# A state-space layer and a routed low-rank projection on one core: the set-up re-ordered, pair 0's projection put among the weights

## What is computed

```python
# x: (64 sequences, 64 heads, 1024 samples); per head a kernel K of 1024 samples from 64 modes
dtA = (-exp(log_A_real) + 1j * A_imag) * exp(log_dt)[:, None]
K   = 2 * einsum('hn,hnl->hl', Cc * (exp(dtA) - 1) / A, exp(dtA * arange(L))).real
y   = (causal convolution of (x * mask) with K) + x * mask * D      # mask: sample < length of the sequence
x   = x + y * mask
# then per token (sequence, head): 1024 -> 1024, plus a low-rank part of 8 experts of rank 16
logits  = x @ Wr.T + 5 * onehot(language)
gates   = softmax of the two largest logits, 0 elsewhere
out = x + x @ W.T + 2 * einsum('bter,bte,eor->bto', x @ A.T, gates, B)
```

## Time and profile before

| | us |
|---|---|
| the runs, median of 3 | 696.15 (695.85 to 696.51) |
| the profiled execution | 695.72 |
| its span, first to last instruction | 693.9 |
| PE busy | 645.8 (93%) |
| DVE busy | 490.0 (71%) |
| ACT busy | 467.8 (67%) |
| POOL busy | 20.4 (3%) |

### The profile page before, as it was taken

One profiled execution on the slowest core, in us unless ns is written; L12 is line 12 of the kernel. 1 busy time (PEld: TensorE's weight loads), 2 busy tenths in 40 slices (PEclk: granted clock), 3 DMA queues, 4 the chain that ended last, 5 costly groups with the idle time before them and its releaser, 6 DMA issues.

```text
span 693.9 us, 12598 instructions
## 1 busy us (share of the span) xinstructions
PE 645.8 (93%) x3621; PEld 615.2 (89%) x3621; DVE 490.0 (71%) x1531; ACT 467.8 (67%) x973; POOL 20.4 (3%) x46
## 2 busy tenths in 40 slices
PE   3364999999999999999999999999999999999997
PEld 2353899999999999999999999999999999999997
DVE  8876567777776767777776767777776767777621
ACT  4784577677768677677768677777768677675411
POOL 2000000000000000000000000000000000000000
PEclk9875899999999999999999999999999999999999
DMA  7123023222123233223123233223123223221112
GB/s 241 49 69 89 11 68 70 54 52 68 32 67 68 68 68 68 53 53 68 31 68 68 68 68 68 53 53 68 31 68 68 68 68 68 53 53 39 31 32 60
DMA packets 22869, 43.36 MB, mean 62 GB/s; under 512 B 8104, under 2 KB 13512, under 8 KB 22856
## 3 DMA queue, kind: packets, MB, share of 16 engines
q1 hardware_dynamic: 17576, 26.42, 17.1%
q10 hardware_dynamic: 5280, 16.78, 9.5%
HBM read 26.35 MB, written 16.84 MB: 62 GB/s over the span
## 4 chain that ended last, share of the span: by engine, by line
DVE 36%; ACT 25%; issue 18%; PE 13%; ACTq 6%; DMA 2%; DVEq 1%; SPq 0%
DVE state L783 17%; PE pmg L1104 9%; ACTq L470 5%; ACT result L488 4%; ACT u_hi L416 4%; ACT turn L379 3%; ACT L393 3%; DVE y_lo L830 3%; ACT swapped L439 2%; ACT Z L405 2%; DVE Z L770 2%; ACT xt L413 2%; DVE c_lo L764 2%; ACT z_swap L398 2%; PE pc L1029 2%
## 5 line engine op out<-in xcount | busy, mean ns | idle before, releaser
L1104 PE MATMUL pmg<-w_hi,y_hi 128*128 128x388 f32 (+1 forms) x768 | 268.7, 350 | 1.7 <-ACT result L488 0.2
L1104 PE MATMUL pmg<-w_hi,y_lo 128*128 128x388 f32 (+1 forms) x768 | 260.1, 339 | 0.0
L1104 PE MATMUL pmg<-w_lo,y_hi 128*128 128x388 f32 (+1 forms) x768 | 259.8, 338 | 0.0
L1104 PEld LDWEIGHTS pmg<-w_hi,y_hi 128*128 128x128 f32 x768 | 144.3, 188 | 7.5 <-ACT result L488 6.5
L1104 PEld LDWEIGHTS pmg<-w_hi,y_lo 128*128 128x128 f32 x768 | 144.6, 188 | 0.2
L1104 PEld LDWEIGHTS pmg<-w_lo,y_hi 128*128 128x128 f32 x768 | 144.2, 188 | 0.0
L439 ACT ACTIVATE swapped<-state 64x128 f32<-64x128 f32 x192 | 59.3, 309 | 67.1 <-DVE state L783 65.7
L783 DVE SCALAR_TENSOR_TENSOR state<-swapped,scan_tab,state 128x192 f32<-128x192 f32 (+1 forms) x240 | 73.8, 349 | 12.1 <-ACT swapped L439 0.2
L812 DVE TENSOR_TENSOR s_lo<-state,s_hi 128x896 fp32r<-128x896 f32 x32 | 35.0, 1093 | 31.5 <-ACT s_hi L461 31.5
L744 DVE TENSOR_TENSOR u_lo<-xt,u_hi 128x1024 fp32r<-128x1024 f32 x32 | 39.2, 1225 | 24.8 <-ACT u_hi L416 24.8
L461 ACT ACTIVATE s_hi<-state 128x896 fp32r<-128x896 f32 x32 | 30.5, 953 | 35.0 <-DVE state L783 35.0
(11 more groups left out here) (195 smaller groups left out, 1068.1 us busy)
## 6 DMA issues: line engine op xcount, KB each, us to landing
rows<-in_x SPq DMA_DIRECT2D x64, 256.0 KB, 5.1
out<-result ACTq DMA_DIRECT2D x62, 256.0 KB, 3.0
toe<-kpad SPq DMA_DIRECT2D x32, 128.0 KB, 4.5
result<-in_L_cond_W SPq DMA_DIRECT2D x5, 512.0 KB, 7.2
rows<-in_L_cond_W SPq DMA_DIRECT2D x2, 512.0 KB, 7.8
result<-in_L_cond_A SPq DMA_DIRECT2D x1, 512.0 KB, 5.8
b_rows<-in_L_cond_B SPq DMA_DIRECT2D x1, 512.0 KB, 7.0
xt<-in_L_cond_W SPq DMA_DIRECT2D x1, 512.0 KB, 8.8
```

Of the source, the lines that this page charges most:

```text
L1104: ins = nc.tensor.matmul(pm[:, n, 0:c1 - c0], y[s][:, c, :], w[:, c, c0:c1], start=(c == 0 and y is y_hi and w is w_hi), stop=(c == CH - 1 ...
```

## The change

The set-up is written anew, and pairs 0 and 1 are taken out of the loop, which now begins with step 2 (`Fori(1, LOOPS)`); from there on all orders are the old ones.

- **Parameters.** The decay's exponential on DVE (14 steps among the others) becomes one exponential of ACT. The far tables move from behind the rows' split to behind the angles of duo 0 on DVE, and `k_first` behind the chunk factors.
- **Kernel samples of pairs 0 and 1.** Two small products of PE (`kernel_row`, with the one-hot columns of `pick`) sum the modes and give a row of samples; ACT copies it; it goes to its own DRAM tensor and comes back as two planes. Duo 0's Z2 is made in halves (`turn_first_powers`, `rotate_first_powers`).
- **Weights.** The order of the tiles is the rank weights, W6, W7, router, W0, W2, W1, W3, W4, W5, B; W2 and W4 are turned in `px`. W0 has its own buffer, W4 comes through `b_sorted`. B is sorted by one copy of ACT in place of eight of POOL, and is last.
- **Pair 0.** Bank 2 starts with three tiles to come, and is cut in 3, 3 and 2 chunks with tiles 7, 8 and 9 in between (`project` takes a range of chunks); bank 0 and bank 1 follow when their tiles are split. `control(0, 1)` moves behind bank 0, tile 10 into bank 1.
- **Peeled steps.** Each engine has a list of its own for the rest of pair 0 and for pair 1. On ACT `finish(0, 0)` stands before `split_rows(0, 2)`, and `finish(0, 1)` between `swap_odd(0, 3, 0)` and `split_obs(0, 4)`.
- **SP** loads rows one step further ahead (`load_rows(b, m + 4)`), and waits in `load_toe` for `tlo_ready` before `k_stored`.

The core of the diff; in the lists (from `store_row(0)` on) lines taken out are not shown again, they stand in the functions above.

```diff
-xt1_rows = xt[1][:, :, :].rearrange("p c t -> p (c t)")
-w_rows = [xt1_rows, rows[0][:, :], result[0][:, :], result[1][:, :], result[0][:, :], result[1][:, :],
-          rows[1][:, :], result[1][:, :]]
-a_rows = result[0][:, :]
+w0_rows = sb("w0_rows", [P, LEN])
 b_rows = sb("b_rows", [P, EXPERTS, 8, RANK])
 b_sorted = sb("b_sorted", [P, 8, EXPERTS, RANK])
+w_rows = [w0_rows[:, :], rows[0][:, :], result[0][:, :], result[1][:, :],
+          b_sorted[:, :, :, :].rearrange("p o e r -> p (o e r)"), result[0][:, :], rows[1][:, :], result[1][:, :]]
+a_rows = result[0][:, :]
...
-TILE = [(A_, in_pm, 0), (B_, in_pc, 0), (W_, in_pm, 6), (W_, in_pc, 0), (WR_, in_pm2, 0), (W_, in_pm, 7),
-        (W_, in_pc, 1), (W_, in_pm, 2), (W_, in_pc, 3), (W_, in_pm, 4), (W_, in_pc, 5)]
+TILE = [(A_, in_pm, 0), (W_, in_pc, 6), (W_, in_pm, 7), (WR_, in_pm2, 0), (W_, in_pm, 0), (W_, in_px, 2),
+        (W_, in_pc, 1), (W_, in_pm, 3), (W_, in_px, 4), (W_, in_pc, 5), (B_, in_pc, 0)]
...
+store_row(0)
+sp.wait_ge(pad_stored, 64)
+load_toe_rows(0)
+store_row(1)
+load_toe_rows(1)
+load_w(4)
+sp.dma_start(b_rows[:, :, :, :].rearrange("p e o r -> p e (o r)"),
+             B.rearrange("e (p o) r -> p e (o r)", o=8)).then_inc(b_in, 16)
 sp.wait_ge(wt_full, w_tile(7) + 1)
 load_w(3)
+sp.wait_ge(px_full, 2)
+load_rows(0, 3)
+sp.wait_ge(wt_full, w_tile(2) + 1)
+load_w(5)
 sp.wait_ge(wt_full, w_tile(1) + 1)
 load_rows(0, 2)
 store_kernel(0, 2)
...
+def turn_first_powers(j):
+    for h in (2 * j, 2 * j + 1):
+        ins = nc.scalar.activation(Z2[:, h, :], Z[:, h, :], ACT.Copy, scale=gen_scalar(C2_RE, 0, h, False))
+    ins.then_inc((z_half, z_swapped)[j], 1)
+def kernel_row(j):
+    act.wait_ge(row_full, j + 1)
+    nc.scalar.activation(k_row[j][:, :], row_psum[:, j, :], ACT.Copy).then_inc(k_ready, 1)
+def sort_b():
+    act.wait_ge(b_in, 16)
+    act.wait_ge(wt_full, w_tile(4) + 1)
+    nc.scalar.activation(b_sorted[:, :, :, :].rearrange("p o e r -> p e o r"), b_rows[:, :, :, :], ACT.Copy
+                         ).then_inc(b_ready, 1)
...
+turn_first_powers(0)
+split_ctr(0, 0)
+kernel_row(0)
+turn_first_powers(1)
 weight(0)
 turns_of(1, False)
+weight(1)
 copy_states(0, 0, first=True)
+split_ctr(0, 1)
+kernel_row(1)
 swap_odd(0, 0, 0)
+split_obs(0, 0, first=True)
 swap_odd(0, 0, 1)
+waves(1)
+swap_odd(0, 0, 2)
+split_toe(0, 0, toe_rows_back, first=True)
+split_states(0, 0, first=True)
 weight(2)
+split_rows(0, 1, first=True)
 weight(3)
 split_obs(0, 1, first=True)
+split_y(0, 0)
 weight(4)
 weight(5)
+weight(6)
+magnitudes(1, False, reused=True)
+weight(7)
+ratios(0, 0)
+weight(8)
+swap_powers(1)
+sort_b()
+weight(9)
+turn_powers(1, False)
+weight(10)
 copy_states(0, 1)
 swap_odd(0, 1, 0)
+split_gated(0, 0)
 swap_odd(0, 1, 1)
 swap_odd(0, 1, 2)
+split_toe(0, 1, toe_rows_back)
+split_states(0, 1)
+finish(0, 0)
+split_rows(0, 2)
 split_ctr(0, 2)
 split_obs(0, 2)
+split_y(0, 1)
+copy_states(0, 2)
+act.wait_ge(gen_staged, 1)
+turns_of(None, True)
+swap_odd(0, 2, 0)
+magnitudes(None, True)
+swap_odd(0, 2, 1)
+swap_odd(0, 2, 2)
+split_toe(0, 2)
+split_states(0, 2)
+split_ctr(0, 3)
+split_obs(0, 3)
+waves(2)
+split_rows(0, 3)
+swap_powers(2)
+turn_powers(2, True)
+nc.scalar.activation(warm[:, :], phase[:, 0:1], ACT.Exp)
+ratios(0, 1)
+split_y(0, 2)
+split_ctr(0, 4)
+split_gated(0, 1)
+copy_states(0, 3)
+swap_odd(0, 3, 0)
+finish(0, 1)
+split_obs(0, 4)
+swap_odd(0, 3, 1)
+split_toe(0, 3)
+swap_odd(0, 3, 2)
+split_states(0, 3)
+split_rows(0, 4)
...
+def rotate_first_powers(j):
+    dve.wait_ge((z_half, z_swapped)[j], 1)
+    for h in (2 * j, 2 * j + 1):
+        ins = vec.scalar_tensor_tensor(out=Z2[:, h, :], in0=z_swap[:, h, :],
+                                       scalar=gen_scalar(C2_IM, 0, h, False), in1=Z2[:, h, :],
+                                       op0=ALU.mult, op1=ALU.add)
+    ins.then_inc((z2_half, z2_ready)[j], 1)
...
+split_rows(0, 0)
+rotate_first_powers(0)
+split_ctr(0, 0, kernel=False)
+rotate_first_powers(1)
+low_weight(0)
+angles(1)
+low_weight(1)
+split_ctr(0, 1, kernel=False)
+dve.wait_ge(chunk_ready, 1)
+scanning = scan_states(0, 0, staged=False)
+next(scanning)
+next(scanning)
+split_obs(0, 0)
+next(scanning)
+next(scanning)
+split_toe(0, 0, toe_rows_back)
+split_states(0, 0)
+dve.wait_ge(small_in, 48)
+dve.wait_ge(consts, 4)
+vec.tensor_copy(len_f[:, :], len_i[:, :]).then_inc(masks, 1)
+vec.tensor_copy(lang_f[:, :], lang_i[:, :]).then_inc(masks, 1)
 dve.wait_ge(masks, 2)
 vec.tensor_tensor(valid[:, :, :], sample_no[:, :].unsqueeze(2).to_broadcast([P, CH, SEQS]),
                   len_f[:, :].unsqueeze(1).to_broadcast([P, CH, SEQS]), ALU.is_lt).then_inc(masks, 1)
 vec.tensor_scalar(bias[:, :], expert_no[:, :], lang_f[:, :], LANG_BIAS, ALU.is_equal, ALU.mult
                   ).then_inc(masks, 1)
 low_weight(2)
 low_weight(3)
+split_obs(0, 1)
+dve.wait_ge(masks, 4)
+merge(0, 0)
 split_rows(0, 1)
+split_y(0, 0)
 low_weight(4)
 low_weight(5)
+low_weight(6)
 powers(1)
+low_weight(7)
+route(0, 0)
+low_weight(8)
+low_weight(9)
+rotate_powers(1, False)
+low_weight(10)
 scanning = scan_states(0, 1, staged=False)
 next(scanning)
+next(scanning)
+split_gated(0, 0)
+next(scanning)
+next(scanning)
+split_toe(0, 1, toe_rows_back)
+split_states(0, 1)
+split_rows(0, 2)
 split_ctr(0, 2)
 split_obs(0, 2)
+merge(0, 1)
+split_y(0, 1)
+angles(2)
+dve.wait_ge(scan_staged, 1)
+scanning = scan_states(0, 2)
+next(scanning)
+next(scanning)
+next(scanning)
+next(scanning)
+split_toe(0, 2)
+split_states(0, 2)
+split_ctr(0, 3)
+split_obs(0, 3)
+split_rows(0, 3)
+powers(2)
+rotate_powers(2, True)
+route(0, 1)
+merge(0, 2)
+split_y(0, 2)
+split_ctr(0, 4)
+split_gated(0, 1)
+scanning = scan_states(0, 3)
+next(scanning)
+split_obs(0, 4)
+next(scanning)
+split_toe(0, 3)
+next(scanning)
+next(scanning)
+split_states(0, 3)
+split_rows(0, 4)
...
+def kernel_row(j):
+    pe.wait_ge((z2_half, z2_ready)[j], 1)
+    if j:
+        pe.wait_ge(k_ready, j)
+    for h in range(2):
+        ins = nc.tensor.matmul(row_psum[:, j, :], pick[:, h, :], Z2[:, 2 * j + h, :], start=h == 0,
+                               stop=h == 1, skip_group_check=True)
+    ins.then_inc(row_full, 1)
...
+def last_bank(b, m, tables_split, rows_ahead):
+    project(b, m, 2, 0, 2)
+    turn_gates(b, m, tables_split)
+    project(b, m, 2, 2, 5)
+    if rows_ahead:
+        turn_rows(b, m + 3)
+    project(b, m, 2, 5, 7)
+    add_loras(b, m)
+    project(b, m, 2, 7, 8)
+    add_lora(BANK_ORDER[2])
...
+kernel_row(0)
 pe.wait_ge(prm_ready, 2)
+turn_powers(0, 0, first=True)
 control(0, 0)
+kernel_row(1)
+pe.wait_ge(clo_ready, 1)
 turn_powers(0, 1)
 turn_weight(2)
+turn_rows(0, 1)
+pe.wait_ge(k_ready, 2)
 turn_weight(3)
+pe.wait_ge(wlo_ready, 2)
+convolve(0, 0, first=True)
 turn_weight(4)
+pe.wait_ge(uhi_ready, 2)
 turn_weight(5)
 pe.wait_ge(merged, 1)
 turn_weight(6)
+wait_y(0, 0)
+pe.wait_ge(wlo_ready, 4)
+project(0, 0, 0, 0, 3)
+turn_weight(7)
+project(0, 0, 0, 3, 6)
+turn_weight(8)
+project(0, 0, 0, 6, 8)
+turn_weight(9)
+pe.wait_ge(wlo_ready, w_tile(3) + 1)
+project(0, 0, 1)
+pe.wait_ge(wlo_ready, w_tile(4) + 1)
+control(0, 1)
+pe.wait_ge(wlo_ready, w_tile(5) + 1)
+project(0, 0, 2, 0, 2)
+turn_weight(10)
+turn_gates(0, 0, 2)
+project(0, 0, 2, 2, 5)
+turn_rows(0, 2)
+project(0, 0, 2, 5, 7)
+pe.wait_ge(wlo_ready, WTILES)
+add_loras(0, 0)
+project(0, 0, 2, 7, 8)
+add_lora(BANK_ORDER[2])
 turn_powers(0, 2)
+convolve(0, 1)
+control(0, 2)
+wait_y(0, 1)
+project(0, 1, 0)
+pe.wait_ge(clo_ready, 3)
+turn_powers(0, 3)
+project(0, 1, 1, 0, 5)
+turn_rows(0, 3)
+project(0, 1, 1, 5, 8)
+convolve(0, 2)
+control(0, 3)
+turn_powers(0, 4)
+last_bank(0, 1, 5, True)
...
```

More of the change, by code:

```diff
@@ L111, in cond_resid_kernel @@
         toe_back = [bass.AP(t[:, :, :].tensor, 2 * P - 2, [[2 * P, P], [1, 2], [-2, P]]) for t in toe]
+        k_row = [sb(f"k_row{s}", [2, P]) for s in range(2)]
+        toe_rows = [bass.AP(t[:, :, :].tensor, 0, [[2 * P, P], [P, 2], [1, P]]) for t in toe]
+        toe_rows_back = [bass.AP(t[:, :, :].tensor, P - 1, [[2 * P, P], [P, 2], [-1, P]]) for t in toe]
+        pick = sb("pick", [P, 2, 2])
         DT_RE, TURNS, C2_RE, C2_IM, A_RE, AA_RE, A_IM, AA_IM = range(8)
@@ L314, in _ @@
                     step(b, m)
-            step(LOOPS, 0)
+            step(LOOPS, 0, rows_left=False)
         @block.gpsimd
@@ L510, in _ @@
             waves(0)
+            act.wait_ge(far_step, 5)
+            for q in range(2):
+                nc.scalar.activation(far_wave[:, q, :, :], far_wave[:, q, :, :], ACT.Sin, scale=-TWO_PI,
+                                     bias=phase[:, 2 + q:3 + q]).then_inc(far_waved, 1)
             act.wait_ge(px_full, 1)
@@ L619, in _ @@
             dve.wait_ge(tables, 1)
+            for h in range(2):
+                vec.memset(pick[0:MODES, h, h:h + 1], 1.0)
             vec.tensor_scalar(phase[:, 2:4], phase[:, 0:2], TWO_PI, None, ALU.mult).then_inc(tables, 1)
@@ L1128, in _ @@
+            convolve(0, 0, first=True)
             turn_weight(4)
+            pe.wait_ge(uhi_ready, 2)
```

(30 more changed lines are left out.)

283 lines of the change are left out of this document (106 added, 177 removed).

## The result

The changed kernel takes 706.73 us, median of 4 runs (706.13 to 707.92), beside 696.33 us of 4 runs of the kernel before (695.85 to 697.55): ratio 1.0149, interval 1.013 to 1.0168. It is slower by 10.4 us. The forecast was 706.8.

A forecast was written before the change was run, and what follows sets the result against it. PE was taken to set the pace from 74.7 us; pair 2's first bank at 124.6 against 115.9 gave +8.7, the clock 2, sum +10.7 on 695.7: 706.4, with 0.4 to the median 706.8 us, range 698.8 to 713.0.

The forecast's parts named there:

- A: Set-up to the split of pair 0: about 5 us earlier, near half at 35.2 instead of 40.6, y split at 43.7.
- terms without a row: Costs no profile row priced: kernel-row product and its copy, taken 0.6 us; ACT's sort of B, taken 1.0.
- B: Pair 0's banks among the weights, 43.7 to 68.3 us: a PE stall of 3.0, pair 0 done 25.6 us earlier.
- C: From there to pair 1's first bank, at 79.9 us: a lead of 12.8 us over the kernel before.
- D: Peeled step 1 up to the rows of pair 3: a serial chain of ACT and DVE ending at 95.5 us.
- E: From the rows of pair 3 to pair 2's first bank: a serial chain to 124.6 us, +8.7 us at full clock.
- The clock, 2 us: PE's clock halving after gaps before the gates' turn and convolution 3: 2 us added, ends 0 and 4.
- Rival 3: PE cold all through step 1, its 23 us of work taking twice as long: about 715 us, chance 0.06.
- Rival 1: Peeled steps keep up and the 12.8 us lead stays, if PE stalls under 12.8 us: 683.4 us, chance 0.09.

The follow-up runs named there:

- experiment 7: experiment 6 with the kernel samples of pairs 0 and 1 made and sent the old way, as a column through `kpad`: 681.64 us, ratio 0.9787.
- experiment 1: The changed kernel with `finish(0, 1)` on ACT moved behind the rows of pair 4 (`split_rows(0, 4)`): 701.44 us, ratio 1.0063.
- experiment 2: The changed kernel with the tails of ACT's and DVE's peeled lists replaced by the loop's own step, PE's list kept: 695.63 us, ratio 0.999.
- experiment 4: The changed kernel with idle PE products in five gaps: 705.62 us; again with 11 instead of 24 before the gates' turn: 706.74 us.
- experiment 3: experiment 2 with `finish(0, 0)` on ACT also moved, behind the control and observation splits: 693.34 us, ratio 0.9954.
- experiment 6: experiment 5 with PE's wait for B's tile moved from before the loop into the step, before bank 0: 681.11 us, ratio 0.9777.
- experiment 5: The changed kernel's new set-up, but all 11 tiles before the first step, no early banks, loop from step 0: 685.89 us, ratio 0.9838.

## Why the prediction was right

- **A** (near half 35.2, bank 43.7): 34.95 and 43.87. Right; but I gave the rows of samples a share in it, and experiment 7 shows that they have none. Of the terms without a row, the products of one row of samples took 1.01 us and its copy 0.25, where I took 0.6 together, and the sort of B took 1.06, where I took 1.0. I also read the earlier trace rows a little wrong: the row is below 9 in slices 2 to 5 only, and not in the first or the last one. Nothing hangs on that.
- **B** (pair 0 done at 68.3, stall 3.0): stall 3.3, end 69.2. The 0.9 is a term that I had left out: the clock fell in that stall already (0.84 in the window at 63.0), the turn of rows took 1.94 us for 1.0, and the first few products behind it ran at half clock. None of the 0.9 reached the next mark.
- **C** (79.9): 80.03. Right, and the bank that began there ran at half clock till 84.
- **D** (95.5): 96.07. The Trainium skill, "ScalarE: Activation LUTs", section "What ACT_TABLE_LOAD costs", would have added a drain of 1.38 us. In the trace ACT's load of 1.28 us ends at 92.17 and the waves start at 92.19, so there is none to see:

```profile
90.89 1.28 ACT L415 ACT_TABLE_LOAD   x1
92.19 0.63 ACT L415 ACTIVATE angle<-angle 128x512 f32<-128x512 f32 x1
```

- **E** (99.9, 106.4, `zo_hi` at 115.4, bank at 124.6 plus the clock): 100.40, 106.91, 116.43, 127.05. The chain is right and experiments 1 and 2 show it by taking it away. The gates' turn is 0.5 us late, as all since D; pair 1's last bank then took 0.6 longer than 7.1 us, with half clock until 111.
- **The clock, 2 us.** As a total it fits: the far products took 2.4 us for 1.2, pair 1's end took 0.6 more, and from the first bank of pair 2 on, which began at half clock, it is 0.2 more than before. Its place was too narrow: I named two gaps, and the clock was low from 63 to 66.7 us, 77 to 84, 98 to 111 and 117 to 128. Rival 3, which put PE at half clock all through step 1, went too far as well: from 84 to 96 us the granted clock was 1.00. The rule of the Trainium skill, "TensorE: Matmul & The Clock Gate", section "HAM oscillation — how this bites in real kernels", agrees with these rows in kind: the clock fell four times, each time in or soon after a wait. But the price of it was small here, since what PE does at half speed lay mostly beside the chain of ACT and DVE.
- **Rival 1** decides at PE stalls of 12.8 us, and I counted 21.5 at full clock, 23.5 with the clock. By the marks the lead at 80.03 was 96.48 - 80.03 - 3.8 = 12.65, the lag at the end 11.1: 23.8 us were lost between. Only 1.94 + 2.86 + 3.89 + 5.54 + 1.56 = 15.8 of them are idle time in the brackets; the other 8.0 are mostly PE at half clock (by the distances of its products about 7.5), where it works while it would otherwise have waited. So the sum is right and its split was not: slow products stand in the place of waits, which is also why experiment 4 gained nothing by warming some of them. Experiment 2 has brackets of 1.5, 2.9 and 2.9 there, and its time comes out even with the kernel before.
- **The agreement to 0.1 us is in part luck.** The first bank of pair 2 came 0.45 us later than the sum with the clock has it (127.05 for 126.6), the profiled execution took 706.97 for 706.4, and the 2 us of the clock were a choice between 0 and 4. What the record supports is the mechanism and the size within about 1 us.
- **What I did not foresee** is the price of pair 0's early banks themselves. With the loop's order in step 1 they still end at 693.3, while the same set-up without them takes 681.1. The first bank of pair 2 starts at 113.96 in experiment 3 and at 101.46 in experiment 6, so the 12.6 us of span between them are lost before it: PE's waits are 15.1 us against 8.1, and the clock is 0.81 against 1.00 from 80 to 102 us. Where the waits come from, DVE's timelines tell; the first row of the scan of pair 1 in the kernel before, in the changed kernel and in experiment 5:

```profile
49.11 0.74 DVE L783 SCALAR_TENSOR_TENSOR state<-state,tab,px 128x192 f32<-128x192 f32 x2 [0.25 <-ACT swapped L439]
```

```profile
63.14 0.73 DVE L870 SCALAR_TENSOR_TENSOR state<-state,tab,px 128x192 f32<-128x192 f32 x2
```

```profile
46.79 0.73 DVE L837 SCALAR_TENSOR_TENSOR state<-state,tab,px 128x192 f32<-128x192 f32 x2
```

The early banks put this scan back by 14 us against the kernel before, since PE does `control(0, 1)` behind two of them and ACT and DVE split B's tile in front of it. The prediction had the scan's end right (68.7) and did not ask when it had ended before. That this and the half clock are the whole 12 us was not taken apart: between experiments 3 and 6 the lists of the three engines in this stretch and the wait for B's tile differ too, and no run kept the early banks with `control(0, 1)` in front of them. Nor was the set-up's gain divided among its edits other than the rows of samples.

## What to carry to other kernels

Work that was moved forward on the busiest engine brought no time here, since the engines that feed its next piece did not get forward too; before moving such work, follow their chain to the first point where the loop runs by itself, and compare that one mark. Where each engine works down one list, try the loop's own order first for the hand-written entry (experiment 2), and put stores, for which hardly anybody waits, behind every split that somebody does wait for (experiments 1 and 3). And a wait for all of a set belongs where its last member is used: here that alone brought 5.4 us of span.

## What the runs showed of the hardware

The store of the kernel samples as two rows was back sooner than as a column, of the same 1 KB. SP issues the transfer back only when the store has landed, so its timeline shows how long that took; first experiment 6, then experiment 7:

```profile
22.46 0.24 SPq L277 DMA_DIRECT2D kpad_rows<-k_row  x1
23.61 0.40 SPq L282 DMA_DIRECT2D toe<-kpad_rows  x1
```

```profile
21.73 0.36 SPq L264 DMA_DIRECT2D kpad<-k_col  x1
24.59 0.33 SPq L272 DMA_DIRECT2D toe<-kpad  x1
```

1.15 us from issue to issue for the row, 2.86 for the column. For pair 0 SP waits in experiment 6 for other small stores as well; for pair 1, where it waits for this store alone, it is 1.10 and 2.92. The row pays for it with a later start, as its products and copy come first. The clock also fell after shorter idle stretches than I had reckoned with: near the end of one of 3.3 us at 63 us in the changed kernel, and in the gap of 2.8 us inside convolution 3, in experiment 4 (the rows above) and likewise in experiment 1: its clock was 1.00 in the windows from 113 to 117.5 us and 0.50 from 119.8.
